# FP4 feed-forward on one Trainium2 core: h's block normalisation moved to GpSimd, x's magic numbers to ScalarE, the next gate-up product put ahead of the rounding

## What is computed

```
x = x + 0.5 * ffn(layernorm(x))
x = x + attention(layernorm(x))        # 16 heads of 8, causal
x = x + 0.5 * ffn(layernorm(x))

def fp4_quant_dequant(x):              # blocks of 16 along the last dim
    scale = max(max(|block|) / 6, 1e-12)
    xn = block / scale
    q = nearest of {0, .5, 1, 1.5, 2, 3, 4, 6} to |xn|, with xn's sign
    return q * scale
def fp4_linear(x, w): return fp4_quant_dequant(x) @ fp4_quant_dequant(w).T
def ffn(x):
    h = silu(fp4_linear(x, w_gate)) * fp4_linear(x, w_up)     # 352 wide
    return fp4_linear(h, w_down)
```

## Time and profile before

| | us |
|---|---|
| median of 3 runs | 599.87 |
| the runs | 596.04 to 605.29 |
| the profiled execution, its time | 596.57 |
| its span | 594.9 |
| VectorE busy in the span | 432.9 (73%) |
| TensorE matmuls | 453.9 (76%) |
| ScalarE | 310.7 (52%) |
| GpSimd | 250.2 (42%) |

### The profile page before, as it was taken

The page is one execution under the profiler, slowest core; times in us unless marked ns, Lnnn a source line. Parts: engine busy times, 40 slices in busy tenths (PEclk is TensorE's granted clock), DMA queues, the critical chain, the costliest instruction groups (busy, mean ns, idle before and its releaser), DMA issues.

```text
span 594.9 us, 13110 instructions
## 1 busy us (share of the span) xinstructions
PE 453.9 (76%) x3673; PEld 321.8 (54%) x3689; DVE 432.9 (73%) x1212; ACT 310.7 (52%) x745; POOL 250.2 (42%) x448
## 2 busy tenths in 40 slices
PE   0667877784687988879878898788798667777785
PEld 0335655563564656556555566565575445555564
DVE  6699999995256666667556676566662899999983
ACT  2245455543225555656546666466557445555553
POOL 4344444443114453454434545444435344444431
PEclk9989899999677888998889989899978979999999
DMA  7000000001344323344134443234400000000000
GB/s 201 9 0 3 0 0 0 0 0 36 80 118 115 89 81 88 99 118 109 46 81 116 116 109 85 74 87 112 117 2 3 2 8 20 18 18 18 18 18 28
DMA packets 28408, 33.31 MB, mean 56 GB/s; under 512 B 1668, under 2 KB 25172, under 8 KB 26068
## 3 DMA queue, kind: packets, MB, share of 16 engines
q1 hardware_dynamic: 28371, 32.86, 20.6%
HBM read 21.91 MB, written 10.49 MB: 54 GB/s over the span
## 4 chain that ended last, share of the span: by engine, by line
DVE 25%; PE 20%; DMA 20%; issue 19%; ACT 5%; POOL 4%; SPq 3%; DVEq 1%; POOLq 0%; ACTq 0%
DMA k_stack<-k_parts 15%; DMA k_parts<-qk_parts 4%; PE bank L979 3%; PE bank L937 3%; PE bank L914 3%; DVE hq_amax L618 2%; DVE f_h L740 2%; PE bank L965 2%; POOL qk_parts L425 2%; DVE hq_grid L652 2%; PE bank L934 2%; SPq L350 2%; SPq L358 1%; PE bank L851 1%; DVE hq_normed L629 1%
## 5 line engine op out<-in xcount | busy, mean ns | idle before, releaser
L771 DVE TENSOR_REDUCE nm<-bank 128x2 f32<-128x512 f32 (+1 forms) x192 | 129.1, 686 | 87.8 <-PE bank L937 85.1
L440 POOL TENSOR_SCALAR_AFFINE_SELECT probs<-probs 128x256 f32<-128x256 f32 (+1 forms) x192 | 91.6, 485 | 76.7 <-ACT probs L563 72.7
L563 ACT ACTIVATE probs<-bank 128x512 f32<-128x512 f32 x192 | 108.5, 596 | 28.3 <-PE bank L965 26.9
L937 PE MATMUL bank<-k_stack,q_stack 72*128 72x256 bf16 (+1 forms) x512 | 80.0, 262 | 40.4 <-DMA k_stack<-k_parts 40.4
L878 PE MATMUL bank<-wdT,f_hT 128*128 128x128 f32 (+1 forms) x384 | 61.2, 298 | 34.5 <-ACT f_hT L508 34.1
L878 PEld LDWEIGHTS bank<-wdT,f_hT 128*128 128x128 f32 (+1 forms) x384 | 50.2, 199 | 45.1 <-ACT f_hT L508 29.2
L851 PE MATMUL bank<-wguT,f_xT 128*128 128x352 f32 x128 | 55.5, 517 | 21.2 <-ACT f_xT L490 21.2
L965 PE MATMUL bank<-q_stack,k_stack 75*128 75x256 bf16 (+1 forms) x512 | 68.8, 253 | 2.3 <-ACT probs L563 1.7
L934 PE MATMUL bank<-causal,ident_bf 128*128 128x256 bf16 (+1 forms) x176 | 57.9, 329 | 4.5 <-DVE nm L771 4.3
L471 ACT ACTIVATE hq_magic<-hq_exps 128x704 bf16<-128x704 bf16 x32 | 25.3, 790 | 66.9 <-DVE hq_exps L638 66.9
L937 PEld LDWEIGHTS bank<-k_stack,q_stack 72*128 72x128 bf16 x512 | 48.8, 105 | 13.6 <-issue 4.8
(11 more groups left out here) (113 smaller groups left out, 960.3 us busy)
## 6 DMA issues: line engine op xcount, KB each, us to landing
q_stack<-q_parts SPq DMA_DIRECT2D x16, 576.0 KB
k_stack<-k_parts SPq DMA_DIRECT2D x16, 576.0 KB
q_parts<-qk_parts SPq DMA_DIRECT2D x16, 192.0 KB, 2.1
k_parts<-qk_parts SPq DMA_DIRECT2D x16, 192.0 KB, 2.4
k_parts<-qk_parts SPq DMA_DIRECT2D x16, 128.0 KB, 2.3
out_dram<-x_all SPq DMA_DIRECT2D x16, 128.0 KB, 1.8
q_stack<-nmT SPq DMA_DIRECT2D x16, 24.0 KB
x_all<-in_L_attn_X_dram SPq DMA_DIRECT2D x1, 256.0 KB, 3.0
```

The costliest lines, as they stand in the source:

```text
L440: nc.gpsimd.affine_select(out=v, in_=v, compare_op=ALU.is_ge, fill=0.0, base=0, pattern=[[0, heads], [1, P]], channel_multiplier=-1).then_ ...
L563: nc.scalar.activation(probs[:, c, :], ps[:, :], ACT.Exp, scale=SCALE).then_inc(done, 1)
L771: nc.vector.tensor_reduce(nm[:, j, h0:h0 + n], ps[:, :].rearrange("p (h k) -> p h k", h=n), AX_X, ALU.max, negate=True).then_inc(done, 1)
L937: last = nc.tensor.matmul(ps[:, keys * h:keys * h + keys], q_stack[0:QROWS, s, h0 + h, P * j:P * j + P], k_stack[0:QROWS, s, h0 + h, 0:key ...
```

## The change

- The new order is `xT gu0 hT0 gu1 hq hn lnS hT1 xo lnA ho lnE he h0 lnN h1 xq xr hr dn`.
- hq on VectorE (`invert_both`) now makes amax, scale and reciprocal of h and x, then `below` (h's reciprocal times the constant just below one, 128 x 44), then x's normalised blocks. h's normalised blocks are made by GpSimd in the new step hn: one tensor_tensor multiply, 128 x 704, f_h times `below` spread over the blocks.
- VectorE's later steps: xo makes x's odd and exps, ho h's odd (it waits for GpSimd's normed), he h's exps; hr has the four sums and grids only.
- x's magic numbers are made by ScalarE in a new step xo, 128 x 256, which in its program stands after hT1; h's magic stands behind it, in he, and both now follow the silus and the copies of h.
- h0 and h1 stand between he and hr. They wait for the last batch's normed instead of its grid.

```diff
--- before.py
+++ after.py
@@ -36,7 +36,7 @@
 EXP_BITS = 0x4080
 MAGIC_MUL, MAGIC_ADD = 48.0, 80.0
 QSTEPS = 8
-QEXPS = 6
+QINV, QNORMED, QODD, QEXPS, QSUM = 3, 4, 5, 6, 7
@@ -45,12 +45,13 @@
 FFN_LAG = {step: lag for lag, steps in enumerate((
     "lnS lnA lnE lnN",
-    "xq xr",
+    "xq xo xr",
     "xT gu0 h0 gu1 h1",
-    "hq hr",
+    "hq hn ho he hr",
     "hT0 hT1 dn",
 )) for step in steps.split()}
-FFN_ORDER = "xT lnS hq lnA lnE xq gu0 xr hr h0 hT0 gu1 lnN hT1 dn h1".split()
+FFN_ORDER = "xT gu0 hT0 gu1 hq hn lnS hT1 xo lnA ho lnE he h0 lnN h1 xq xr hr dn".split()
+FFN_AHEAD = FFN_LAG["hq"] - FFN_LAG["xq"]
 FFN_UNROLL = 2
@@ -222,6 +223,8 @@
             def __init__(self, n, m, turns):
                 self.m, self.blocks = m, m // BLOCK
                 self.amax, self.inv = (sb(f"{n}_{k}", [P, m // BLOCK]) for k in ("amax", "inv"))
+                self.below = sb(f"{n}_below", [P, m // BLOCK])
+                self.below_ready = sem(f"{n}_below_ready")
                 self.scale = sb(f"{n}_scale", [P, turns, m // BLOCK])
                 self.normed = sb(f"{n}_normed", [P, m])
                 self.odd, self.exps, self.magic, self.sum = (
@@ -231,6 +234,9 @@
                 self.step = sem(f"{n}_step")
                 self.magic_ready = sem(f"{n}_magic_ready")
                 self.ready = sem(f"{n}_ready")
+            def blocks_of(self, values):
+                return values.rearrange("p (n k) -> p n k", k=BLOCK)
         class NormBuffers:
             def __init__(self, n, turns):
@@ -412,12 +418,19 @@
                         pool.wait_ge(f_xT_filled, b + base - 1)
                     rescale(xquant, b + base, s)
+                def h_normed(b, s, it):
+                    q, n = hquant, b + base
+                    pool.wait_ge(q.below_ready, n + 1)
+                    nc.gpsimd.tensor_tensor(
+                        q.blocks_of(q.normed[:, :]), q.blocks_of(f_h[:, :, :].rearrange("p j i -> p (j i)")),
+                        q.below[:, :].unsqueeze(2).to_broadcast([P, q.blocks, BLOCK]), ALU.mult).then_inc(q.step, 1)
                 def h_rescale(b, s, it):
                     if base or not first(b, 2):
                         pool.wait_ge(hT_filled[NT - 1], b + base - 1)
                     rescale(hquant, b + base, s)
-                steps = {"lnE": lambda b, s, it: inverse_std(fln, b + base), "xr": x_rescale, "hr": h_rescale}
+                steps = {"lnE": lambda b, s, it: inverse_std(fln, b + base), "xr": x_rescale, "hn": h_normed, "hr": h_rescale}
                 return Pipeline(FFN_ORDER, FFN_LAG, FFN_UNROLL, NB, steps)
             def third_parts(b, s, it):
@@ -471,9 +484,15 @@
                 nc.scalar.activation(q.magic[:, :], q.exps[:, :], ACT.Copy, scale=MAGIC_MUL, bias=MAGIC_ADD).then_inc(q.magic_ready, 1)
             def ffn(base, ps):
-                def magic_weights(b, s, it):
+                def magic_alone(b, s, it):
                     if not base and first(b, 1):
                         magic(wquant, 0)
+                    if first(b, FFN_AHEAD):
+                        magic(xquant, b + base)
+                def magic_x(b, s, it):
+                    if not first(b, FFN_AHEAD):
+                        magic(xquant, b + base)
                 def x_norm(b, s, it):
                     norm_apply(fln, s, b + base, b, (xquant.step, QSTEPS * (b + base - 1)) if base or not first(b, 2) else None)
@@ -508,8 +527,8 @@
                         nc.scalar.copy(f_hT[0:KLAST, KT - 1, cols], ps.hT[j][0:KLAST, (KT - 1) * P:KT * P]).then_inc(hT_read[j], 1)
                     return f
-                steps = {"xT": x_copy, "lnN": x_norm, "xq": magic_weights,
-                         "hq": lambda b, s, it: magic(hquant, b + base), "dn": down}
+                steps = {"xT": x_copy, "lnN": x_norm, "xq": magic_alone, "xo": magic_x,
+                         "he": lambda b, s, it: magic(hquant, b + base), "dn": down}
                 for j in range(NT):
                     steps.update({f"gu{j}": gate_silu(j), f"hT{j}": h_copy(j)})
                 return Pipeline(FFN_ORDER, FFN_LAG, FFN_UNROLL, NB, steps)
@@ -601,54 +620,54 @@
                 nc.vector.memset(w_raw[KLAST:P, (KT * n + KT - 1) * P:(KT * n + KT) * P], 0.0).then_inc(w_cleared, 1)
             nc.vector.memset(w_raw[:, 2 * KT * P + I:3 * KT * P], 0.0).then_inc(w_cleared, 1)
-            def quantise(*jobs):
-                def wait(q, n, k):
-                    dve.wait_ge(q.step, QSTEPS * n + k)
-                def blocks(q, src):
-                    return src.rearrange("p (n k) -> p n k", k=BLOCK)
+            def wait_step(q, n, k):
+                dve.wait_ge(q.step, QSTEPS * n + k)
+            def block_inverse(*jobs):
                 for q, s, n, src, released in jobs:
-                    nc.vector.tensor_reduce(q.amax[:, :], blocks(q, src), AX_X, ALU.max, apply_absolute_value=True).then_inc(q.step, 1)
+                    nc.vector.tensor_reduce(q.amax[:, :], q.blocks_of(src), AX_X, ALU.max, apply_absolute_value=True).then_inc(q.step, 1)
                 for q, s, n, src, released in jobs:
-                    wait(q, n, 1)
+                    wait_step(q, n, 1)
                     if released:
                         dve.wait_ge(*released)
                     nc.vector.tensor_scalar(q.scale[:, s, :], q.amax[:, :], 1.0 / 6.0, SCALE_MIN, ALU.mult, ALU.max).then_inc(q.step, 1)
                 for q, s, n, src, released in jobs:
-                    wait(q, n, 2)
+                    wait_step(q, n, 2)
                     nc.vector.reciprocal(q.inv[:, :], q.scale[:, s, :]).then_inc(q.step, 1)
+            def normalise_blocks(*jobs):
                 for q, s, n, src, released in jobs:
-                    wait(q, n, 3)
-                    nc.vector.scalar_tensor_tensor(out=blocks(q, q.normed[:, :]), in0=blocks(q, src), scalar=BELOW_ONE,
+                    wait_step(q, n, QINV)
+                    nc.vector.scalar_tensor_tensor(out=q.blocks_of(q.normed[:, :]), in0=q.blocks_of(src), scalar=BELOW_ONE,
                                                    in1=q.inv[:, :].unsqueeze(2).to_broadcast([P, q.blocks, BLOCK]),
                                                    op0=ALU.mult, op1=ALU.mult).then_inc(q.step, 1)
+            def take_odd(q, n):
+                wait_step(q, n, QNORMED)
+                upper = q.normed[:, :].bitcast(I16).rearrange("p (n two) -> p n two", two=2)[:, :, 1]
+                nc.vector.tensor_scalar(q.odd[:, :].bitcast(I16), upper, 1, None, ALU.bitwise_or).then_inc(q.step, 1)
+            def take_exps(q, n):
+                wait_step(q, n, QODD)
+                nc.vector.tensor_scalar(q.exps[:, :].bitcast(I16), q.odd[:, :].bitcast(I16), EXP_BITS, None,
+                                        ALU.bitwise_and).then_inc(q.step, 1)
+            def quantise(*jobs):
+                block_inverse(*jobs)
+                normalise_blocks(*jobs)
                 for q, s, n, src, released in jobs:
-                    wait(q, n, 4)
-                    upper = q.normed[:, :].bitcast(I16).rearrange("p (n two) -> p n two", two=2)[:, :, 1]
-                    nc.vector.tensor_scalar(q.odd[:, :].bitcast(I16), upper, 1, None, ALU.bitwise_or).then_inc(q.step, 1)
+                    take_odd(q, n)
                 for q, s, n, src, released in jobs:
-                    wait(q, n, 5)
-                    nc.vector.tensor_scalar(q.exps[:, :].bitcast(I16), q.odd[:, :].bitcast(I16), EXP_BITS, None,
-                                            ALU.bitwise_and).then_inc(q.step, 1)
+                    take_exps(q, n)
             def round_fp4(*jobs):
-                for q, s, n in jobs:
-                    if q is xquant:
-                        dve.wait_ge(q.step, QSTEPS * n + QEXPS)
-                        nc.vector.tensor_scalar(q.magic[:, :], q.exps[:, :], MAGIC_MUL, MAGIC_ADD, ALU.mult, ALU.add).then_inc(q.magic_ready, 1)
                 for q, s, n in jobs:
                     dve.wait_ge(q.magic_ready, n + 1)
                     nc.vector.tensor_tensor(q.sum[:, :], q.odd[:, :], q.magic[:, :], ALU.add).then_inc(q.step, 1)
                 for q, s, n in jobs:
-                    dve.wait_ge(q.step, QSTEPS * n + QEXPS + 1)
+                    wait_step(q, n, QSUM)
                     nc.vector.tensor_tensor(q.grid[:, s, :], q.sum[:, :], q.magic[:, :], ALU.subtract).then_inc(q.step, 1)
@@ -701,48 +720,61 @@
                     return (hquant, s, b + base, f_h[:, :, :].rearrange("p j i -> p (j i)"),
                             (hquant.ready, b + base - 1) if base or not first(b, 2) else None)
-                ahead = FFN_LAG["hq"] - FFN_LAG["xq"]
                 def quantise_x(b, s, it):
                     if not base and first(b, 1):
                         quantise_weights(x_job(b, s))
-                    elif first(b, ahead):
+                    elif first(b, FFN_AHEAD):
                         quantise(x_job(b, s))
```

(29 more changed lines are left out.)

## The result

| | before | after |
|---|---|---|
| median, us | 597.95 (4 runs) | 642.54 (4 runs) |
| the runs | 595.52 to 605.29 | 638.39 to 653.5 |
| ratio, 95% interval | | 1.074 (1.064 to 1.084) |

The changed kernel is 44.6 us slower. The sign of the forecast was right; the size was twice the forecast 22.9, and the time lies above the range.

A forecast was written before the change was run, and what follows sets the result against it. VectorE was taken to bound both feed-forwards. 28 batch intervals at +0.56 us (15.7), plus 5.0 for starts and 2.2 for the end, gave 22.9 on the profiled 596.57: 619.5, raised to 621 for the median; range 604 to 635.

The forecast's parts named there:

- Parts 1 and 2: VectorE's own work falls from 7.40 to 6.32 us a batch; GpSimd's hn product takes 1.65 us.
- Part 1: VectorE's list in a feed-forward batch: its own work falls from 7.40 to 6.32 us.
- Part 3: GpSimd's rescale and hn hold VectorE at h's scale (0.60 us) and x's odd (0.94); batch 7.96 us.
- ring alone: Rival: GpSimd does not hold VectorE, the ring sets 7.4 to 7.6 us a batch, total 604 to 609; chance 0.15.
- Starts from nothing: Rival: VectorE's held scale and x's odd need their whole durations after GpSimd ends; total 632 us, chance 0.08.
- Part 4: Second bound through all engines: 7.61 us a batch, hidden below 7.96; low clock costs up to 2.6 each time.
- The ring: Per-batch dependency loop from x's grid through GpSimd, TensorE, ScalarE and back to VectorE's sums and x's grid: 7.61 us.
- Part 5: Ends of phases: x(1) quantised after the silu wait, 5.0 us for two phases; 2.2 us at the kernel's end.
- Faster: Rival: the ring closes in under 6.9 us and GpSimd holds nobody; VectorE's 6.3 to 6.4 rules, 576 us, chance 0.04.

The follow-up runs named there:

- e3: The changed kernel with h's normed blocks made on VectorE again, without hn on GpSimd and without `below`; 637.91 us.
- e6: e3 with the statistics, aggregate and variance (lnS, lnA, lnE) moved ahead of hq; 649.94 us.
- e8: e6 with xq ahead of he, hT1 behind he and three extra matmuls a batch in TensorE's wait for x; 623.45 us.
- e1: The changed kernel with three extra matmuls a batch, their result overwritten, in TensorE's wait for x; 619.35 us.
- e2: The changed kernel with step xq moved between lnE and he; 631.07 us.
- e10: The changed kernel, hn still on GpSimd, with xq ahead of he, hT1 behind he and three extra matmuls a batch; 617.31 us.
- e7: The kernel before with one wait relaxed: VectorE's h product waits for the last batch's normed, not its grid; 591.55 us, ratio 0.993.
- e4: The changed kernel with x's magic made on VectorE at the head of the sums, not on ScalarE; 644.16 us.
- e5: The changed kernel with hT1 moved behind he, so ScalarE makes both magics before hT1's copies; 637.83 us.
- e9: e8 with lnA and lnE back behind the normed blocks, only lnS ahead of hq; 614.38 us.
- e11: e9 without the three extra matmuls; 609.36 us.
- e12: e11 with one extra matmul a batch; 608.90 us.

## Why the prediction was right in sign and wrong in size

- **Parts 1 and 2, right.** VectorE is busy for 7.65 us in a full-clock batch; less the two holds (0.50 and 0.80, below) that is 6.35, against 6.32 in Part 1. hn took 1.51 us (forecast 1.65, bounds 1.38 to 1.99; where nothing of VectorE meets it, at the phase's end, 1.39). The Trainium skill's GPSIMD Engine Reference, section "Elementwise — side-by-side cycle accounting", measures 4497 ns for a two-input f32 tensor_tensor of 2048 numbers; scaled to 704 that is 1.55, an estimate. This trace has 1.51 for hn where VectorE meets it, and 1.39, a tenth less than the estimate, where nothing does.
- **Part 3, right, a little too dear.** Forecast: scale loses 0.60, x's odd 0.94, the batch takes 7.96. Measured: 0.50, 0.80, and 7.83. So 28 x 0.43 = 12 us instead of 15.7. e3 (x's odd free without hn) and e6 (scale free behind the rescale) show each hold with its holder, and the "ring alone" rival fell: both instructions are held. The Trainium skill's SBUF — State Buffer, section "Who interferes with whom", has the rule of the exclusive pair, and the traces agree with it in after, e3, e6 and e8. The price of its section "A bandwidth-pool intuition that's wrong", with which the forecast would have come to 639 and so near to the median, does not hold here: the held scale ended 0.04 after its holder and x's odd 0.16, not 0.115 + 0.18 and 0.115 + 0.29. The nearness of 639 is chance; the missing 20 us were elsewhere. "Starts from nothing" fell by the same rows.
- **Part 4, wrong, the largest error.** The ring was seen, and its 7.61 at full clock is hidden under 7.83, as forecast. The step that failed is "I put 0 to 5 us for it into the range and nothing into the sum". That sentence priced low stretches as if they would stay as rare as they were before (a mean clock of 0.96 over 13 intervals), and no step asked whether the change makes them more frequent. But in the changed order TensorE waits 1.6 to 1.7 us in one place, where before it waited 0.80 and 0.94 apart, and the clock now fell in about every second batch. Each such batch costs 9.21 - 7.82 = 1.4 us, because the ring, whose TensorE part lengthens, has both magics in it now, and at low clock VectorE's work no longer covers it. e1 gives 20 to 23 us back, against 0 to 5 in the forecast. The price of one stretch (up to 2.6) was written down; how often one falls was not worked out.
- **Part 5, wrong by half or more.** x(1) behind the products cost 3.0 us in the first phase, where the forecast took 2.5. What it missed is the other engine in the same move: xq is also ScalarE's step for the weights' magic, and the move put it behind lnN, whose input comes from GpSimd. To that I put the other 5.1 of the 8.1 in all; e2, which brings the weights' magic 5.4 earlier, mends both at once, so no run separates the two. The second phase lost 2.4, so both starts cost 10.5 against 5.0 forecast, and e2's trace gives 10.1 of it back. The rule to count every instruction that a moved step issues was applied to VectorE alone. The end was too cheap as well: from the 15th amax of the second feed-forward to the last instruction after takes 5.9 us more than before (4.3 in e1, without the low clock), against 2.2 forecast; that was not taken apart.
- **The sum, by place.** The profiled spans differ by 651.8 - 594.9 = 56.9 us. The first amax comes 8.1 later; the first 14 intervals of the two feed-forwards are longer by 16.9 and 17.8; the end has 5.9; the remaining 8.1 lie in the attention and the change of phase before it, and the medians, 44.6 apart, don't bear them out. Of the 34.7 in the intervals 12 are the holds and 2.4 the second start, which leaves 20 for the low clock; e1 takes 19.6 away there. So 12 (15.7 forecast), 20 (0 forecast), 10.5 (5.0) and 5.9 (2.2): 48, a few us over the difference of the medians, as this profile is the longest of its runs. The causes don't simply add when they are mended together: e10 has two mended and its filling in the ring.
- **"Faster", 0.04, fell**; its two conditions failed: GpSimd does hold VectorE, and no kernel here has a steady batch under 7.2 us (e7, the shortest, 7.22 to 7.27).

What stays open is what makes the clock fall. Filling TensorE's 1.6 us wait raises it: e1 runs at mean clocks of 0.931 to 0.942, after at 0.869 to 0.891. Over all their runs the kernels fall into three groups. In after, e2, e3, e4, e5 and e6, where TensorE's longest wait is 1.2 us or more in most batches, the mean is 0.869 to 0.902. In e1, e8, e9 and e10, with three extra matmuls a batch, it is 0.925 to 0.947. Before, e7, e11 and e12 lie between, 0.896 to 0.945, with longest waits near 1 us, and within that group nothing here orders them: before and e11 have nearly the same waits and, in full-clock batches, nearly the same busy share (5.7 to 5.8 of 7.4 us, and 5.8 to 5.9 of 7.47), and yet 0.96 and 0.90 in the first feed-forwards of their profiles. More than that these runs don't show.

## What to carry to other kernels

Before work is moved to GpSimd, lay its new instruction beside VectorE's list and look which tensor_scalar starts inside it: beside GpSimd's large tensor_tensors that one lasted until GpSimd was done, however small it was, and when it was moved the next one took its place. Where a loop goes through all engines, ask what it takes at TensorE's lower clock, and whether the change lengthens TensorE's waits: the clock may fall because of the change, and then the hidden ring is the bound. And follow a moved step through every engine's program, in its first iteration too, where it may carry one-off work such as the weights here.

## What the runs showed of the hardware

- A held instruction costs by its holder, not by its size: 128 x 2 took 0.89 us, 128 x 44 took 0.68 to 0.71, 128 x 256 in int16 took 1.08, each ending 0.02 to 0.16 after GpSimd's instruction. Reductions and the statistics beside the same GpSimd instructions kept their usual durations or nearly so (amax 0.89 against 0.87, the pair of statistics 0.48). VectorE's tensor_tensors on bf16 never started inside one of them here, so of those these traces say nothing.
- Not every instruction of GpSimd holds. Timeline of before, x's scale inside GpSimd's power on 128 x 2:

```profile
19.18 0.69 POOL L397 TENSOR_TENSOR fln_rstd<-fln_var_eps,half_power 128x2 f32<-128x2 f32 x1
19.59 0.17 DVE L623 TENSOR_SCALAR xq_scale<-xq_amax 128x16 f32<-128x16 f32 x1
```

- GpSimd loses too where it starts second: x's rescale took 0.83 instead of 0.61 to 0.63, hn 1.51 instead of 1.39.
- Adding work sped the kernel up: 1.46 us more of matmuls in a wait of TensorE shortened 13 intervals from 112.18 to 102.53 us. Where the wait was too short for it (e9, e10), the same filling put x's transpose off by 1.1 us.
- An aggregate directly behind its own statistics sat idle for 0.27 us (e8), which nobody sees while something stands between them.
